# A four-stage batch pipeline on one core: the adapter of the next batch as a fifth stage, and a scratch written for two loads instead of six

## The reference, cut to what matters

```
x = x + relu(x @ Wd_b.T + bd) @ Wu_b.T + bu      # L0: Wd_b, Wu_b = W + 0.1 * (h @ Wdd.T + bdd) for batch b
x = (layernorm(x) * w + bias + tanh(...)) * w + bias      # L1
h = layernorm(x) * g1 + b1;  q, k, v = h @ W_qkv.T + b_qkv      # L2
x = x + a1 * (softmax(q k.T / 4) v @ W_o.T + b_o)      # 16 heads of 16
x = x + a2 * (gelu(h2 @ W_f1.T + b_f1) @ W_f2.T + b_f2)
y = quant(val * gelu(gate)) @ ternary(W_down).T + x      # L3
```

## Time and profile before

| | us |
|---|---|
| median of 3 runs | 1076.93 |
| the runs | 1055.72, 1078.08, 1076.93 |
| the profiled execution | 1060.12 |
| its span, first to last instruction | 1057.3 |
| TensorE busy in it | 906.3 (86%) |
| mean granted TensorE clock (share of full speed) | 0.926 |

### The profile page before, as it was taken

The page is one execution under the profiler, slowest core; times in us unless marked ns, Lnnn a source line. Parts: engine busy times, 40 slices in busy tenths (PEclk is TensorE's granted clock), DMA queues, the critical chain, the costliest instruction groups (busy, mean ns, idle before and its releaser), DMA issues.

```text
span 1057.3 us, 17675 instructions
## 1 busy us (share of the span) xinstructions
PE 906.3 (86%) x5852; PEld 656.0 (62%) x5852; DVE 602.0 (57%) x1087; ACT 494.7 (47%) x758; POOL 272.5 (26%) x300
## 2 busy tenths in 40 slices
PE   7983465989898989998998989897989899989996
PEld 3222243758576767676766767675857676767674
DVE  2432456386565747474757575756657475746443
ACT  1321341536364635464463646363636455555542
POOL 3004203060414133231404050505041231411210
PEclk8995675989999989999999999998999999999999
DMA  9886752422525251516151424243251515060000
GB/s 356 275 312 209 179 129 61 90 34 81 86 82 86 69 98 50 115 42 124 41 110 37 111 39 117 44 112 54 81 85 61 106 50 118 1 126 2 27 11 10
DMA packets 50108, 100.86 MB, mean 95 GB/s; under 512 B 7968, under 2 KB 17568, under 8 KB 46832
## 3 DMA queue, kind: packets, MB, share of 16 engines
q1 hardware_dynamic: 50048, 100.18, 37.7%
HBM read 74.38 MB, written 25.25 MB: 94 GB/s over the span
## 4 chain that ended last, share of the span: by engine, by line
PE 59%; DVE 13%; issue 11%; DMA 8%; SPq 5%; POOL 2%; ACT 1%; DVEq 0%; POOLq 0%; ACTq 0%
PE bank L501 20%; DMA Kp<-qk_scratch 7%; PE bank L707 6%; SPq L462 4%; PE pair_t L501 4%; PE pair_s L633 4%; PE pair_s L668 4%; PE bank L679 4%; PE pair_t L654 4%; DVE nmax L1117 3%; PE pair_s L511 3%; PE pair_t L511 3%; DVE hd L1185 2%; PE bank L752 2%; DVE xc L1079 2%
## 5 line engine op out<-in xcount | busy, mean ns | idle before, releaser
L1117 DVE TENSOR_REDUCE nmax<-pair_s 128x4 f32<-128x1024 f32 x128 | 156.4, 1222 | 117.5 <-PE pair_s L633 97.5
L852 ACT ACTIVATE Pr<-pair_t 128x1024 f32<-128x1024 f32 x128 | 131.2, 1025 | 118.1 <-PE pair_t L654 117.9
L707 PE MATMUL bank<-wf,G 128*128 128x256 f32 x512 | 126.9, 392 | 0.0
L633 PE MATMUL pair_s<-Kp,Qp 48*128 48x256 f32 x512 | 67.7, 344 | 63.6 <-DMA Kp<-qk_scratch 38.4
L501 PE MATMUL bank<-wup_hi,hD_hi 128*128 128x512 f32 x256 | 112.1, 438 | 7.6 <-ACT gl L896 3.7
L1338 POOL TENSOR_TENSOR x<-x,xcr 128x512 f32<-128x512 f32 x16 | 20.5, 1280 | 360.7 <-DVE x L1175 360.7
L501 PE MATMUL bank<-wup_hi,hD_lo 128*128 128x512 f32 x256 | 105.0, 410 | 0.0
L501 PE MATMUL bank<-wup_lo,hD_hi 128*128 128x512 f32 x256 | 104.7, 409 | 0.0
L707 PEld LDWEIGHTS bank<-wf,G 128*128 128x128 f32 x512 | 93.0, 191 | 17.2 <-issue 0.8
L633 PEld LDWEIGHTS pair_s<-Kp,Qp 48*128 48x128 f32 x512 | 41.8, 200 | 93.7 <-issue 57.3
L896 ACT ACTIVATE gl<-bank,rsD 128x512 f32<-128x512 f32 x64 | 44.1, 689 | 88.4 <-PE bank L501 88.1
(11 more groups left out here) (170 smaller groups left out, 2010.8 us busy)
## 6 DMA issues: line engine op xcount, KB each, us to landing
hyp<-in_hyper SPq DMA_DIRECT2D x16, 1024.0 KB, 7.9
Qp<-qk_scratch SPq DMA_DIRECT2D x96, 128.0 KB, 4.2
Kp<-qk_scratch SPq DMA_DIRECT2D x96, 128.0 KB, 6.7
tC<-rows_scratch SPq DMA_DIRECT2D x16, 384.0 KB, 5.6
cur_scratch<-gen SPq DMA_DIRECT2D x16, 256.0 KB, 7.6
xT_t<-in_xT SPq DMA_DIRECT2D x16, 256.0 KB, 4.2
x_t<-in_x SPq DMA_DIRECT2D x16, 256.0 KB, 4.3
cur<-cur_scratch SPq DMA_DIRECT2D x16, 256.0 KB, 2.7
```

The costliest lines, as they stand in the source:

```text
L633: mm = pe.matmul(pair_s[:, half, r * L:(r + 1) * L], Qp[lo:lo + KQ, 1 - par, p, r * P:(r + 1) * P], Kp[lo:lo + KQ, 1 - par, p, :], start=T ...
L707: mm = pe.matmul(bank[5][:, r * D:(r + 1) * D], G[:, k, r * P:(r + 1) * P], wf2[:, k, :], start=k == 0, stop=k == FT - 1)
L852: act.activation(Pr[:, p % 4, :, :].rearrange("p a n -> p (a n)"), pair_t[:, :, :].rearrange("p a n -> p (a n)"), ACT.Exp, scale=DH ** -0. ...
L1117: dve.tensor_reduce(nmax[:, n % 2, :, p % GP, :], pair_s[:, :, :].rearrange("p a (r n) -> p a r n", r=RT), AX.X, ALU.max, negate=True).the ...
```

## The change

1. Stage Z: adapter, residual, first statistics and first 1/sqrt of batch t+1 run in turn t, on all engines; stage A begins at its first normalisation. A turn -1 ("ahead") does Z of batch 0. The unrolled turns are now -1 to 3 and 12 to 18 (before: 0 to 3 and 14 to 18), and turn 15 has a list of its own ("fifteen").
2. The lists of every turn are rewritten. `C.proj` now stands ahead of `B.s0` on DVE.
3. `A.k` writes bank 4, like q and v, and waits for q's low part; `A.v` waits for k's.
4. `qk_scratch` becomes (2, 128, 3, 512): each row's three parts lie side by side. The high part is stored twice by one DMA, so a store of it is 512 KB. Each of q and k is loaded by two DMAs of 48 partitions.
5. The maxima are split in two parts before the transposition (new DVE slice `B.p`, on 128x8 numbers), transposed together, copied once, and sent by two DMAs instead of four.
6. `tA` is loaded apart from the adapter weights: `A.load` loads tA of t+1, `Z.load` loads cur, xT_t and x_t of t+2.
7. `normalise` uses a DVE instruction of another form: scalar_tensor_tensor with the reciprocal as a broadcast tensor.

```diff
   "full": {
     "SP": """
-        C.tc B.m0 A.load A.qs B.m1 A.ks D.y0 A.ql A.kl D.y1""".split(),
+        C.tc B.m0 A.qs B.m1 D.y0 A.load A.ql A.ks A.kl D.y1 Z.load""".split(),
     "PE": """
+        B.s0 C.proj D.u0 B.s1 D.u1 C.ht B.s2 D.u2 B.s3 C.f0 C.f1 B.m0 A.ht C.f2 B.s4 C.f3 D.u3 B.s5 B.t0 A.q B.s6 C.g0 B.t1 B.s7 C.g1 B.t2 A.k B.m1 B.t3 C.g2 D.qt0 B.o0 A.v D.y0 B.t4 D.qt1 B.o1 Z.down B.t5 D.y1 Z.up B.t6 C.g3 B.t7 B.o2 B.o3 C.xt""".split(),
     "DVE": """
-        B.s0 C.proj A.up B.s1 C.ln A.lna D.u0 C.lnb B.s2 ...
+        C.proj B.s0 C.ln D.u0 A.lna C.lnb B.s1 D.u1 B.s2 A.ln B.s3 B.p0 A.lnb B.m0 D.quant0 D.u2 B.s4 B.s5 D.u3 B.s6 A.q B.s7 B.p1 B.m1 A.k D.quant1 D.y0 B.o1 D.y1 Z.up C.g3 B.o3 Z.cur""".split(),
   "fifteen": {
     "SP": """
+        C.tc B.m0 A.qs B.m1 A.ks D.y0 A.kl A.ql A.load D.y1""".split(),
...
+            def store_part(w, rows, part, stored):
+                dst = qk_scratch[w, :, rows, :]
+                src = part[:, :, :].rearrange("p a b -> p (a b)").unsqueeze(1).to_broadcast([P, dst.shape[1], 2 * L])
+                sp.dma_start(dst, src.bitcast(F32)).then_inc(stored, 16)
+            def load_heads(dst, w, par, arrived):
+                for half in range(2):
+                    sp.dma_start(dst[64 * half:64 * half + KQ, par, :, :].rearrange("p (j c) n -> p j (c n)", j=4).bitcast(F32),
+                                 qk_scratch[w, 64 * half:64 * half + 64].rearrange("(j d) r n -> (d r) j n", j=4)).then_inc(arrived, 16)
...
                 def a_k():
-                    if with_c:
-                        pe.wait_ge(act_c, at(ACT_C, "gelu7", c))
-                    else:
-                        past(pe, dve_a, DVE_A, "klo1", a, 1)
+                    pe.wait_ge(dve_a, at(DVE_A, "qlo1", a))
...
                 def normalise(buf, mv, rs, sem_):
                     for r in range(RT):
-                        dve.tensor_scalar(buf[:, r, :], buf[:, r, :], mv[:, r, 0:1], rs[:, 1, r:r + 1],
-                                          ALU.subtract, ALU.mult).then_inc(sem_, 1)
+                        dve.scalar_tensor_tensor(buf[:, r, :], buf[:, r, :], mv[:, r, 0:1], rs[:, 1, r:r + 1].to_broadcast([P, D]),
+                                                 ALU.subtract, ALU.mult).then_inc(sem_, 1)
```

More of the change, by code:

```diff
@@ L38 @@
 KM = KQ + 2
-PE_A = ["down", "up", "ht", "q", "k", "v"]
+PE_Z = ["down", "up"]
+PE_A = ["ht", "q", "k", "v"]
 PE_S = [f"s{p}" for p in range(NP)]
@@ L85 @@
     "SP": """
-        A.load A.qs A.ks A.ql A.kl""".split(),
+        A.qs A.ks A.ql A.kl A.load Z.load""".split(),
     "PE": """
-        A.down A.up A.ht A.q A.k A.v""".split(),
+        A.ht A.q A.k A.v Z.down Z.up""".split(),
     "ACT": """
-        A.down A.ht A.q A.k A.v""".split(),
+        A.ht A.q A.k A.v Z.down""".split(),
     "DVE": """
-        A.up A.lna A.ln A.lnb A.cur A.q A.k""".split(),
+        A.lna A.ln A.lnb A.q A.k Z.up Z.cur""".split(),
     "POOL": """
-        A.down A.up A.lna A.ln A.ht""".split(),
+        A.lna A.ln A.ht Z.down Z.up""".split(),
   },
@@ L155, with order @@
   },
-}
-OWN_ORDER = {0: "zero", 1: "one", 2: "two", NB: "drain", NB + 1: "late", NB + 2: "last"}
-def order(slices, a, b, c, d):
-    on = {"A": a, "B": b, "C": c, "D": d}
+  "ahead": {
+    "SP": """
+        Z.load""".split(),
+    "PE": """
+        Z.down Z.up""".split(),
+    "ACT": """
+        Z.down""".split(),
+    "DVE": """
+        Z.up Z.cur""".split(),
+    "POOL": """
+        Z.down Z.up""".split(),
+  },
+  "fifteen": {
+    "SP": """
+        C.tc B.m0 A.qs B.m1 A.ks D.y0 A.kl A.ql A.load D.y1""".split(),
+    "PE": """
+        B.s0 C.proj D.u0 B.s1 D.u1 C.ht B.s2 B.s3 C.f0 D.u2 B.m0 C.f1 D.u3 B.s4 A.ht C.f2 B.s5 C.f3 D.qt0 B.s6 B.t0 A.q C.g0 B.s7 B.t1 C.g1 B.t2 B.o0 B.m1 C.g2 A.k B.t3 C.g3 B.t4 B.o1 D.y0 B.t5 D.qt1 B.t6 D.y1 B.t7 B.o2 B.o3 C.xt A.v""".split(),
+    "ACT": """
+        D.u0 D.u1 C.ht C.f0 D.u2 D.u3 C.f1 A.ht C.f2 C.f3 B.t0 B.t1 A.q B.t2 D.qt0 B.t3 A.k B.t4 B.t5 D.qt1 B.t6 B.t7 C.xt A.v""".split(),
+    "DVE": """
+        B.s0 C.proj A.lna C.ln D.u0 C.lnb B.s1 D.u1 B.s2 D.quant0 B.s3 A.ln B.p0 B.m0 A.lnb D.u2 B.s4 D.u3 B.s5 B.s6 D.quant1 B.s7 B.p1 A.q B.m1 A.k B.o1 D.y0 C.g3 D.y1 B.o3""".split(),
+    "POOL": """
+        C.proj C.ln A.lna C.ht A.ln A.ht C.g3 C.xt""".split(),
+  },
+}
+OWN_ORDER = {-1: "ahead", 0: "zero", 1: "one", 2: "two", NB - 1: "fifteen", NB: "drain", NB + 1: "late", NB + 2: "last"}
+def order(slices, z, a, b, c, d):
+    on = {"Z": z, "A": a, "B": b, "C": c, "D": d}
     out = []
@@ L344, in alone @@
                 body(t, t % 2, slices[first:])
-            full = order(ORDERS["full"][engine], True, True, True, True)
-            for t in range(4):
+            full = order(ORDERS["full"][engine], True, True, True, True, True)
+            for t in range(-1, 4):
                 alone(t)
-            with eng.Fori(4, NB - 2, 2) as t:
+            with eng.Fori(4, NB - 4, 2) as t:
                 body(t, 0, full)
                 body(t + 1, 1, full)
-            for t in range(NB - 2, NB + 3):
+            for t in range(NB - 4, NB + 3):
                 alone(t)
```

275 lines of the change are left out of this document (142 added, 133 removed).

## The result

The changed kernel takes 1145.32 us (median of 4 runs, 1143.37 to 1148.67); the kernel before took 1071.47 beside it (4 runs, 1055.72 to 1078.08). The ratio is 1.081, interval [1.076, 1.087]: slower by 8%. I had said 1084, with a range up to 1120. The forecast was a loss of 0.7%, which I had called too small to tell from none; the measured loss is ten times that, and it lies outside the range.

What follows compares the result with a forecast made beforehand. PE was taken as the bound, with a wait for the K tile in every turn. Turns 3 to 14 gave +15 us, other parts -7.5; the sum, +7.5, set on the median 1076.9 gave 1084 us, range 1043 to 1120.

Steps and rivals of the forecast that it cites:

- E: Full turn, from its start to the end of `ys` on DVE: forecast 41.55 us.
- K: Full turn, from the end of `ys` to the next `B.s0`: forecast 14.9 us, against 14.1 before.
- a late tC and a long `C.lnb`: First 10 us of a full turn: a loss between 0.15 and 2.9 us, taken as 1.45.
- rival D: K tile wait at `B.s0` gone, PE alone sets the turn: 51.15 us a turn, 1016 in all; chance 0.07.
- a load of 48 partitions lies between them; the middle is 3.7 us: Q and K loads: each 786 KB tile takes 3.7 us (212 GB/s), between 5.4 and 2.05.
- Rival C: Load rate stays at 145 GB/s because of the DRAM source: +3.4 us per turn, 1125 in all; chance 0.2.
- in turns that start at the low clock I reckon +0.5: Low-clock full turns: +0.5 us, against +1.9 at full clock; half and half gives +1.2.
- near 5 us: PE's wait for the K tile before `B.s0` in full-clock turns: grows to near 5 us.
- The start: Turns ahead of turn 3: -4.5 us for adapter work leaving turn 2's head, -1 for turn 0's loads.
- the bank: k in bank 4, waiting for q's low part: at nothing; without that cover 1 us.
- Turn 15: K stores ahead of `D.y0` and no stage Z: -2 us, between -4 and +1.
- The new layout's saved issues: Load issues on SP, twelve of 0.45 us to four of 0.5: hidden behind transfers that kept the engines busy.

## Why the prediction was wrong

*The form of the model was right.* A turn is E + K, the K stores lie in the chain from `ys`, PE's own work is what is left when the loads are hidden. E at full clock was forecast at 41.55; the kernel with early loads, whose turns 4 to 14 run at full clock, has 41.65. That match is in part luck: the forecast had 1.45 for a late tC and a long `C.lnb`, tC is not late there, and in its place PE waits for oT (0.81 in turn 6), which the sum didn't have. The turn without a wait was forecast at 51.15 us (rival D); it is 52.2.

*The step that failed: "a load of 48 partitions lies between them; the middle is 3.7 us".* In turn 5 K is 18.0 us against 14.9. From `ys` to the landing of the K stores I had 9.1 us and it took 10.5 (412.40 - 401.94); from there to PE's start 5.7, and it took 7.55. With the 1.4 and 0.6 us at its ends, the K tile took 5.5 us, 143 GB/s, the old rate. I named the bounds 145 and 383 and took the middle between them although the rows gave no reason for it. In the mean of turns 3 to 14 the two pieces are 11.4 and 7.6 us: of the 5.4 us by which the mean turn (61.89) exceeds the forecast at full clock (56.45), 4.2 are K. Rival C had K = 18.3, with the price right and the cause wrong: its "because of the source in DRAM" falls with the load forms, where the target decides. I also read the port rule of the Trainium skill ("SBUF — State Buffer", Door 1) as if 48 partitions spread evenly over eight ports, which made it agree with my value.

*The second step: "in turns that start at the low clock I reckon +0.5".* I let half of the turns start at full clock. A K wait of 7 to 10 us stands in front of every turn, and the granted clock is 0.50 at each start. Its price is the smaller part: E is 42.83 in the mean, against 41.65 in the kernel with early loads. K itself came out at 19.06 in the mean, not 18.0. The loss of a turn was forecast at 1.2 us and is 5.5. The forecast had PE waiting "near 5 us" and should have asked what the low clock of the earlier trace rows then does to each following turn; rival C's 1125 has the same gap, 3.4 a turn.

*The start: forecast -5.5, in fact +16.* Turn 1 is 3.2 us shorter (45.5 against 48.7), where I had -4.5 for the adapter work that leaves turn 2's head. Turn 0 is 9.0 longer. Its trace shows DVE's `Z.cur` of turn -1, which waits for weights of batch 1 until 94.52, ahead of the first normalisation (95.13 against 90.55), and k's high part 4.8 us behind q's (115.41 and 110.63) where they were 1.5 apart: k in the bank of q waits for q's low part. I had set the bank at nothing, from the full turns; in turn 0 the cover named there doesn't exist. Turn 2 is 10.4 us longer: its list stores q only behind the K loads, and the tile of q then is the last to land. I had read SP's list for the full turns alone. These two causes of turn 0 were read in the trace and not tried by themselves.

*Turn 15: forecast -2, in fact +7.* Both loads stand behind `D.y0`, and E there is 48.8 us, against 41.4 before: `D.y0` does come later in this list, as I said, and costs more than K gives back (13.0 against 13.4, where I had near 11). With SP's list put right it was the maxima's DMAs that came late, and with these ahead too the turn takes 57.4, still 2.6 more than before.

*What held.* `C.lnb` shorter, though not by its form alone: 2.15 forecast, 1.92 measured. `C.ht` still waits. tC, forecast late at full clock, is not late in the changed kernel, where no full turn starts at the full clock, nor in the kernel with early loads, where `C.proj` waits for PE too (1.90 us in turn 6); the run with `Z.up` moved shows that the risk was real. The new layout's saved issues are worth nothing, as argued, and its bigger stores cost 0.9 us a turn in the chain. The maxima in two DMAs instead of four, which I put off the path, stay there in the changed kernel; once the loads are early, their place in the queue decides over 6 us.

## What to carry to other kernels

On a queue that is served strictly in order, ask of every DMA that waits for data what stands behind it: here the store of `ys` held back loads whose data had been ready for microseconds, and one move in one list was worth 5%, while the changed kernel, whose list put the stores there too, lost 8%, and most of it by that. Small, urgent transfers go ahead of large ones in the queue, also in the lists for the first and last turns, where the cover that the full turns offer is missing. When a wait of several microseconds comes to stand in front of every turn, count the lower clock of each following turn with it.

## What the runs showed of the hardware

A load's time doesn't follow from the number of partitions alone: with 768 KB in two DMAs, 32 partitions took 5.4 us, 64 took 5.9, 48 took 7.0, and 16 took 8.4; one DMA over 128 took 4.4. The same 48 partitions in eight loads that alternate between the halves took 5.3. Each is three repetitions in one execution.

DMAs of 8 KB issued right behind loads of 768 KB were seen by PE 4.7 us after their issue, though they need none of their data. In the kernel before with early loads, where SP took 3.7 us for the six load issues and 2.7 for the small ones, PE saw the last of the small ones 1.8 us after its issue (381.93 to 383.75).

The change of the DVE instruction's form (a broadcast tensor in place of a scalar operand) made the pair of `A.lna` dearer, 0.87 us instead of 0.73. Beside POOL, in the same order of the work, the pair of `C.lnb` took 1.91 us in the new form in turns 3 to 14, and 1.71 or 2.8 in the old one.
